# Embedding inputs of a small vision tower in five transfers instead of four, and sixteen zero products instead of twenty

## What is computed

```python
p = x.reshape(b, c, nph, PH, npw, PW)
p = p.transpose(0, 2, 4, 1, 3, 5).reshape(b, nph * npw, c * PH * PW)
h = jnp.einsum('bnd,ed->bne', p, Wp) + bp
h = _layernorm(h + attention(h, ...))
h = _layernorm(h + experts(h, ...))
```

## Time and profile before

| | us |
|---|---|
| three timed runs | 118.58, 113.70, 118.98 |
| their median | 118.58 |
| the profiled execution, its own time | 113.86 |
| its span, first to last instruction | 111.7 |
| PE / PEld busy in it | 100.1 / 89.8 |
| DVE / ACT / POOL busy in it | 78.5 / 71.1 / 30.1 |

### The profile page before, as it was taken

How to read it: one execution, slowest core, us unless ns; L and a number is a source line. 1 busy time by engine, 2 the same in 40 slices (tenths; PEclk the granted TensorE clock), 3 DMA queues, 4 the chain that set the end, 5 groups by cost and what they waited for, 6 DMA issues and landing times.

```text
span 111.7 us, 3468 instructions
## 1 busy us (share of the span) xinstructions
PE 100.1 (90%) x1349; PEld 89.8 (80%) x1349; DVE 78.5 (70%) x239; ACT 71.1 (64%) x198; POOL 30.1 (27%) x42
## 2 busy tenths in 40 slices
PE   6989999999999999999999999999959868797940
PEld 4778998998998889789988998998948767684910
DVE  0566909955991887319686888988867779988670
ACT  4678687577659965976865558662366366558260
POOL 4003626699914500000591630000005400000000
PEclk9999999999999999999999999999999999999997
DMA  3999999300000000000000000000000000000202
GB/s 75 355 336 387 414 421 426 126 0 0 6 3 6 3 6 0 0 6 0 0 0 6 0 6 0 0 6 0 3 0 6 3 0 0 6 0 0 65 20 79
DMA packets 4123, 7.73 MB, mean 69 GB/s; under 512 B 1292, under 2 KB 2444, under 8 KB 3980
## 3 DMA queue, kind: packets, MB, share of 16 engines
q1 hardware_dynamic: 3740, 7.24, 17.8%
q10 hardware_dynamic: 368, 0.28, 0.8%
HBM read 7.08 MB, written 0.44 MB: 67 GB/s over the span
## 4 chain that ended last, share of the span: by engine, by line
PE 61%; DVE 16%; ACT 7%; DMA 5%; issue 5%; SPq 3%; DVEq 0%; ACTq 0%
PE proj L920 11%; PE outp L1050 8%; PE score L1005 7%; DMA x_f<-x_t 5%; PE proj L905 4%; PE trans L1029 3%; PE outp L884 3%; PE proj L909 3%; PE proj L906 3%; PE proj L912 3%; PE proj L913 3%; PE proj L1067 2%; ACT ln_ln L562 2%; DVE ln_st L733 2%; PE proj L1072 1%
## 5 line engine op out<-in xcount | busy, mean ns | idle before, releaser
L548 ACT ACTIVATE pt_t<-trans,image_t 108x216 f32<-108x216 f32 (+1 forms) x42 | 14.5, 420 | 1.4 <-PE trans L1029 1.3
L424 POOL TENSOR_TENSOR h_res<-h_hi,bias 128x288 f32<-128x288 f32 x8 | 5.2, 666 | 23.3 <-DVE h_lo L757 23.2
L532 ACT ACTIVATE score<-d_t 128x296 f32<-128x296 f32 (+2 forms) x16 | 6.5, 409 | 6.2 <-DVE d_t L697 6.1
L1005 PE MATMUL score<-k_t,q_t 64*36 64x37 f32 (+1 forms) x416 | 10.3, 196 | 0.0
L1005 PEld LDWEIGHTS score<-k_t,q_t 64*36 64x36 f32 x416 | 9.0, 111 | 1.2 <-issue 0.6
L707 DVE TENSOR_REDUCE sm_t<-score 128x8 f32<-128x288 f32 (+1 forms) x16 | 6.9, 434 | 2.8 <-ACT score L532 2.8
L726 DVE TENSOR_TENSOR x_lo<-outp,x_hi 128x288 fp32r<-128x288 f32 x12 | 5.4, 452 | 4.9 <-ACT x_hi L555 4.8
L694 DVE TENSOR_REDUCE mx_t<-score 128x8 f32<-128x296 f32 (+2 forms) x16 | 7.1, 444 | 2.4 <-PE score L1013 1.4
L920 PE MATMUL proj<-wv_hi,h_hi 128*108 128x384 f32 (+1 forms) x24 | 8.3, 344 | 0.2 <-DVE wv_hi L659 0.2
L562 ACT ACTIVATE ln_ln<-ln_mv,const 108x1 f32<-108x1 f32 (+1 forms) x12 | 3.5, 293 | 7.3 <-DVE ln_mv L736 7.3
L651 DVE TENSOR_TENSOR x_lo<-x_f,x_hi 128x288 fp32r<-128x288 f32 x12 | 6.8, 580 | 1.8 <-ACT x_hi L464 1.8
(11 more groups left out here) (192 smaller groups left out, 335.7 us busy)
## 6 DMA issues: line engine op xcount, KB each, us to landing
ffn_f<-f_w SPq DMA_DIRECT2D x1, 1088.0 KB, 12.1
wqk_f<-w_qk SPq DMA_DIRECT2D x2, 512.0 KB, 7.9
x_f<-x_t SPq DMA_DIRECT2D x2, 432.0 KB, 6.3
wv_f<-w_v SPq DMA_DIRECT2D x1, 768.0 KB, 7.1
wo_f<-w_out SPq DMA_DIRECT2D x1, 768.0 KB, 9.5
x_f<-x_t SPq DMA_DIRECT2D x2, 288.0 KB, 4.8
tw_f<-tok_w SPq DMA_DIRECT2D x2, 256.0 KB, 4.3
wqk_f<-w_qk SPq DMA_DIRECT2D x2, 256.0 KB, 5.6
```

The costliest lines, as they stand in the source:

```text
L548: nc.scalar.activation(pt_t[:, n % 2, 0:tiles, :, i], trans[0:ROWS, 0:tiles, :, 0:TOK], ACT.Copy, scale=image_t[:, i:i + 1]).then_inc(spli ...
L1005: ins = nc.tensor.matmul(s[64 * h:64 * h + TOK, im, 0:width], q, k_t[rows, n % QK_RING, im, 0:width], start=(kind == "attn" and im == 0), ...
```

## The change

`X_PIECES` gets five pieces: chunks 2 and 3 come by themselves, chunks 4 and 5 stay together. Since weights and inputs use the same list, two transfers (weights 256 KB, inputs 288 KB) become four (128, 144, 128, 144 KB). All four are issued by SP. The semaphores follow the list. `WARM_UP` falls from 20 to 16. No other instruction is added, removed or moved, and ACT, DVE and POOL have the same rows in the same order.

```diff
-X_PIECES = [slice(0, 1), slice(1, 2), slice(2, 4), slice(4, 6)]
+X_PIECES = [slice(0, 1), slice(1, 2), slice(2, 3), slice(3, 4), slice(4, 6)]
 X_LATER = [slice(0, 3), slice(3, 6)]
 QK_PIECES = [slice(0, 1), slice(1, 2), slice(2, 4), slice(4, 6)]
-WARM_UP = 20
-ACT_TOK, SP_TOK = (0, 1), (2, 3)
+WARM_UP = 16
+ACT_TOK, SP_TOK = (0, 1), (2, 3, 4)
```

## The result

| | kernel before | changed kernel |
|---|---|---|
| median, 12 runs each | 113.92 us | 114.77 us |
| ratio of the times | | 1.0069, 95% interval 1.0049 to 1.0088 |

A forecast was written before the change was run, and what follows sets the result against it. TensorE is mostly busy; early on the chain waits for group 1's inputs. From 113.86 us: zero products 0, pieces 0, later issue and packets +0.15, giving 114.0; median 118.3, between 117.9 and 118.7; range 113.3 to 119.6.

The forecast's parts named there:

- The chain: First 20 us: from the issue of group 1's inputs at 4.50 us, landing at 10.33, to `em 6` at 11.34.
- The value of the edits in front: Start of group 0: fewer zero products and split chunks 2 and 3 win 0.37 and 0.94 us there, 0 on the chain.
- SP's delay: Two more issues on SP push every later transfer 0.95 us back, group 1's inputs from 4.50 to 5.45.
- The cost of smaller packets: Input transfers: more packets of half the size cost 0.15 us, with bounds 0 and 0.5.
- The engines never run dry, so the landing is set by the bytes ahead, which are the same: DMA at 4.44 us: 0.8 MB still queued, so group 1's landing stays near 10.33; bounds 0 and 0.95 us.
- rival D: Group 1's inputs: the later issue counts fully, +0.95 us, 114.8 or 119.5; chance 0.07.
- last embedding piece: End of group 0: inputs taken at 8.13 us, `em 4` not before 9.2, group 0 through at 10.85.
- list of signs: Profile after: `em 0` at 5.0, `em 2` at 6.75, group 0's last product near 10.55, `em 6` at 11.3 to 11.8.
- The level: Whole execution: timed runs at 113.70 or at 118.58 and 118.98; median expected at the upper one, 118.3.
- the two readings offered for the upper level: Extra time elsewhere gives 118.7; a lower clock lasting on in the beginning gives 117.9.
- Rival B: Start of group 0: TensorE's clock rises later, embedding products 0.240 us apart, +2.3 us, 116.3 or 120.9; chance 0.12.
- Rival C: Group 1's inputs land earlier or TensorE is the bound: 1.4 us less, 112.5 or 117.2; chance 0.06.

The follow-up runs named there:

- e2_sixteen: Kernel before with sixteen zero products in place of twenty, four pieces kept: 114.04 us, ratio 1.0006 to the kernel before.
- e4_act_issues: Changed kernel with the weights of chunks 2 and 3 issued by ACT instead of SP: 113.84 us, ratio 0.9996 to the kernel before.
- e5_wide: Kernel before plus two unused transfers of 128 rows of 8 bytes, issued by SP behind the inputs of chunks 2 and 3: 115.01 us, ratio 1.0082.
- e1_pieces: Changed kernel with twenty zero products instead of sixteen, five pieces kept: 114.82 us, ratio 1.0078 to the kernel before.
- e8_act_four: Kernel before with the weights of chunks 2 and 3 issued by ACT instead of SP: 114.88 us, ratio 1.0088.
- e9_x_first: Changed kernel with group 1's first inputs issued ahead of biases and first query and key weights, chunk 6 earlier on ACT: 115.25 us, 1.0099 to kernel before.
- e3_tiny: Kernel before plus two unused 4 byte transfers issued by SP behind the inputs of chunks 2 and 3: 114.41 us, ratio 1.0044.
- e7_tiny_pool: e3_tiny with POOL's second subtraction held until DVE has made chunk 6's `x_lo`: 114.15 us, ratio 1.0013 to the kernel before.

## Why the prediction was wrong

**What held.** The chain: it runs through group 1's inputs and not through group 0, as read from the earlier trace rows. The value of the edits in front, zero: e2_sixteen, and `em 4` held by the last piece. SP's delay: 0.95 said, 0.97 measured. The cost of smaller packets, 0 to 0.5 with 0.15 taken: e4_act_issues has them and costs at most 0.2% of the time, 0.2 us, by its interval.

**The step that failed** is "The engines never run dry, so the landing is set by the bytes ahead, which are the same", and with it the choice of 0.15 between 0 and 0.95. Measured was nearly the upper end: 0.92 us at the landing for 0.97 at the issue, and 0.8 us in the time. That is rival D, which had a chance of 0.07, at 0.95 us. The same step fails for the last embedding piece, which the prediction left at 8.13 us although it too is issued later: it came 0.6 us later, at 8.74, and `em 4` at 9.82 in place of the 9.2 said. Group 0's last product started at 11.35; the prediction's sum gives 10.7 for it (9.2 + 11 x 0.136), and the 10.55 in its list of signs does not follow from that sum.

The bytes ahead were indeed the same: by the DMA windows 2.89 MB had moved in the kernel before when group 1's inputs landed, and 2.93 MB in the changed one. The rate was not. The engines did run short, and just where the prediction counted 0.8 MB in hand:

```profile
4.00:5.00 1.00, 1.00 (x6) 0.61 (x4) 0.95 (x3) 1.00 (x4) 0.00 (x0) 1.00 0.83 228
```

The last two columns are the busy share of the engines and GB/s; the kernel before has 0.98 and 328 there, and from 4.2 to 4.5 us the changed kernel has 0.54 and 155. One such window is weak evidence by itself: e2_sixteen, which loses nothing, has 0.91 and 280 from 4 to 5 us. One reading in the rows spoke for this. The 0.8 MB "remain" at 4.44 only if everything issued by then could already move. Nothing lands within 2.7 us of its issue, and in the second from 1 to 2 us only 30 KB moved although the first issue stands at 0.74; with about a microsecond between issue and first data, what was issued by about 3.1 (some 0.96 MB) had to be set against the 0.8 moved: nearly nothing left. This is worked out afterwards from rows and was not tested by itself.

Longer windows of DMA show where the rest of the time went; before, changed kernel, e4_act_issues and e5_wide in turn:

```profile
4.00:7.00 3.00, 3.00 (x23) 2.60 (x20) 1.95 (x5) 1.90 (x7) 0.00 (x0) 1.00 1.03 343
7.00:11.00 4.00, 3.51 (x26) 3.21 (x24) 2.84 (x8) 3.38 (x10) 0.88 (x2) 1.00 1.03 369
```

```profile
4.00:7.00 3.00, 3.00 (x17) 2.53 (x15) 2.52 (x7) 2.53 (x8) 0.00 (x0) 1.00 0.95 285
7.00:11.00 4.00, 3.28 (x25) 3.08 (x25) 2.25 (x6) 2.24 (x6) 0.47 (x1) 1.00 0.98 331
```

```profile
7.00:11.00 4.00, 3.71 (x27) 3.32 (x25) 3.17 (x9) 3.64 (x11) 1.07 (x2) 1.00 1.04 391
```

```profile
7.00:11.00 4.00, 4.00 (x32) 4.00 (x31) 2.52 (x7) 2.50 (x7) 0.74 (x1) 1.00 0.94 296
```

The shortfall does not lie in the same place in every run. The changed kernel and e1_pieces both move 285 GB/s from 4 to 7 us, but from 7 to 11 e1_pieces moves 362, nearly as much as the kernel before; e5_wide moves 343 and then 296. So a busy share near 1 does not mean the full rate, and a late issue does not lower the rate in one fixed way.

That the late issue makes the landing late is shown by ten profiled executions together. Issued between 4.0 and 4.5 us, group 1's inputs land between 9.9 and 10.4 (e8_act_four, e9_x_first, e4_act_issues, before, e2_sixteen); issued at 5.0, at 10.3 and 10.9 (e3_tiny, e7_tiny_pool); issued between 5.4 and 5.5, between 11.1 and 11.3 (e5_wide, e1_pieces, the changed kernel). Why the engines move less in e5_wide after 7 us, and whether 0.54 us later costs little or only landed well in e3_tiny, stays open: no run varied the delay in small steps.

The 2.0 us that the prediction quotes from the Trainium skill ("DMA: Bandwidth & Descriptors", section "Anatomy of one DMA") is fitted there to transfers issued from GpSimd. Here SP and ACT issue, so the disagreement that the prediction reads from the trace does not test that figure.

**The level.** The predicted 118.3 rested on a median of three runs, two of them at the upper level. Of twelve, ten were at the lower one; with three runs the prediction could not know this, and 114.0 against 114.77 is the miss that its argument made. Of the two readings offered for the upper level, a low clock at the beginning is not what the profile after shows: its low clock lies at 95 us. Rival B (a later clock at the start) came true in its cause and not in its price: in the profile after the embedding products are 0.24 us apart (5.54, 5.78, 6.02) until about 6.3, the distance that the prediction gives for the lower clock, and so `em 2` starts at 7.35 in place of the 6.75 said; yet TensorE has caught up and is idle before `em 4`, so that cost nothing. The zero products do not decide when the clock rises: in e1_pieces and e5_wide, both with twenty, the products are 0.24 us apart until 7.1, and in e2_sixteen and e9_x_first, both with sixteen, 0.13 us apart from 5.4 on. Rival C fell with the landing.

## What to carry to other kernels

Look at where the chain waits, and at which position of the issuing queue its transfer stands: splitting a transfer that is not on the chain costs each transfer behind it one issue (0.47 us here), and two of them passed on almost in full here (0.92 of 0.97 us). Give the added issues to an engine that is idle (ACT here, which took the loss away; but e8_act_four, with one large transfer moved to ACT, lost 0.9%), or split the transfer that the chain waits for and issue its first part early (chunk 6 here, 0.3% to 0.5% faster). When counting how much work is queued, count only what was issued long enough ago to move.

## What the hardware showed that I had not expected

DVE's subtraction of two SBUF operands took 1.03 us beside POOL's in place of 0.46, and who starts first decides: 0.01 us behind POOL in e3_tiny it waited, 0.04 us ahead of it in the kernel before it did not, and there POOL's own took 1.02 in place of 0.73. That moved `em 6` by half a microsecond. In the changed kernel DVE starts 0.40 us behind POOL's (11.35) and takes 0.65. The Trainium skill ("SBUF — State Buffer", section "Who interferes with whom") states this: a DVE instruction with two SBUF inputs contends with a GpSimd instruction that reads SBUF, over a shared pair of ports that is an exclusive lock. The rows agree: in e3_tiny and in the changed kernel DVE ends 0.32 us behind POOL's end.

TensorE's clock fell at 95 us in the profiled execution of the changed kernel without a long pause: from 90 to 95 us TensorE was busy for 3.56 of 5 us, its longest pause was 0.93 us, and then the granted clock stood at the lower level for about 10 us. That is where this execution's extra 4 us lie; why the clock falls in some executions and not in others stays open.

```profile
90.00:95.00 5.00, 3.56 (x41) 3.09 (x41) 4.10 (x24) 3.50 (x10) 0.00 (x0) 1.00 0.00 0
95.00:105.20 10.20, 9.97 (x106) 9.05 (x101) 6.88 (x23) 3.63 (x12) 0.00 (x0) 0.50 0.01 2
```
